# Gate exponentials moved behind the copy of the fourth power, system matrix and attention weights behind the third correction of the inverse

## The reference, cut to what matters

```python
decay = where(tril, exp(g[:, None] - g[None, :]), 0)
M = where(stril, (k_beta @ k.T) * decay, 0)
T = solve_triangular(eye + M, eye, lower=True)
v_c, k_cumdecay = T @ v_beta, T @ (k_beta * exp(g)[:, None])
# over the chunks, one after the other
attn  = (q_i @ k_i.T) * decay_i
v_new = v_i - kcd_i @ state
out_i = (q_i * exp(g_i)[:, None]) @ state + attn @ v_new
state = state * exp(g_last) + (k_i * exp(g_last - g_i)[:, None]).T @ v_new
```

## Time and profile before

| | |
|---|---|
| median of 3 runs | 3789.3 us (3787.47 to 3796.2) |
| profiled execution, its own time | 3785.71 us |
| its span | 3783.8 us |
| busy: PE, DVE, ACT, POOL | 3344.6, 2453.1, 1968.5, 1505.5 us |
| PE weight loads | 2619.3 us |
| granted TensorE clock, mean over the span | 0.982 of full |
| DMA | 261.53 MB, mean 69 GB/s |

### The profile page before, as it was taken

One profiled execution on the slowest core, in us unless ns is written; L12 is line 12 of the kernel. 1 busy time (PEld: TensorE's weight loads), 2 busy tenths in 40 slices (PEclk: granted clock), 3 DMA queues, 4 the chain that ended last, 5 costly groups with the idle time before them and its releaser, 6 DMA issues. The chain is left out here.

```text
span 3783.8 us, 58251 instructions
## 1 busy us (share of the span) xinstructions
PE 3344.6 (88%) x18978; PEld 2619.3 (69%) x18978; DVE 2453.1 (65%) x5143; ACT 1968.5 (52%) x4746; POOL 1505.5 (40%) x2617
## 2 busy tenths in 40 slices
PE   0114999999999999999999999999999999999987
PEld 0113777777777777777777777777777777777763
DVE  6873566666666666666676666666666666666643
ACT  5762555554555555555555555555555555555531
POOL 9963343433433343434344333434333433334310
PEclk9998999999999999999999999999999999999988
DMA  2013222222222222222222222222222122222202
GB/s 95 33 50 135 70 73 73 72 54 71 75 74 64 67 62 76 75 75 69 53 70 77 72 68 72 54 76 76 73 75 70 51 78 70 74 66 66 56 5 100
DMA packets 291213, 261.53 MB, mean 69 GB/s; under 512 B 220992, under 2 KB 249792, under 8 KB 281152
## 3 DMA queue, kind: packets, MB, share of 16 engines
q1 hardware_dynamic: 281696, 123.60, 13.5%
q10 hardware_dynamic: 9216, 134.22, 9.6%
HBM read 228.11 MB, written 29.62 MB: 68 GB/s over the span
## 5 line engine op out<-in xcount | busy, mean ns | idle before, releaser
L638 PE MATMUL x<-xs,w_high 128*128 128x512 f32 x3072 | 1063.4, 427 | 40.0 <-POOL w_low L1229 34.6
L638 PE MATMUL x<-xs,w_low 128*128 128x512 f32 x1536 | 613.6, 399 | 0.0
L873 ACT ACTIVATE uvec<-rb,cpos 128x128 f32<-128x128 f32 x512 | 160.1, 364 | 868.5 <-PE rb L658 868.5
L638 PEld LDWEIGHTS x<-xs,w_high 128*128 128x128 f32 x3072 | 531.3, 193 | 104.5 <-POOL w_low L1229 35.5
L937 ACT ACTIVATE slot<-lane 128x512 fp32r<-128x512 f32 x640 | 350.8, 608 | 402.1 <-PE lane L764 401.7
L1212 POOL TENSOR_TENSOR block_step<-block_in 64x14 f32<-64x14 f32 (+6 forms) x896 | 229.1, 256 | 506.3 <-DMA block_in<-blocks_dram 385.6
L1244 POOL TENSOR_TENSOR rstd<-rarg,powers 128x8 f32<-128x8 f32 x64 | 105.4, 1647 | 625.8 <-DVE rarg L1046 625.8
L638 PEld LDWEIGHTS x<-xs,w_low 128*128 128x128 f32 x1536 | 292.4, 190 | 67.8
L764 PEld LDWEIGHTS lane<-pinv,slot 128*128 128x128 f32 x1536 | 200.2, 192 | 190.2 <-ACT slot L937 98.9
L1009 DVE SCALAR_TENSOR_TENSOR cacc<-x,cwqk,cacc 128x511 f32<-128x511 f32 (+2 forms) x384 | 281.2, 746 | 44.3 <-ACT cacc L860 22.4
L1009 DVE SCALAR_TENSOR_TENSOR cacc<-x,cwv,cacc 128x511 f32<-128x511 f32 (+2 forms) x384 | 281.7, 747 | 37.9 <-ACT cacc L860 4.1
(11 more groups left out here) (203 smaller groups left out, 7737.2 us busy)
## 6 DMA issues: line engine op xcount, KB each, us to landing
xs<-mix_dram ACTq DMA_DIRECT2D x64, 2048.0 KB, 7.7
gb<-cum_dram SPq DMA_DIRECT2D x128, 256.0 KB, 4.4
w_in<-in_w_qkvz SPq DMA_DIRECT2D x48, 512.0 KB, 4.1
w_out<-in_w_out SPq DMA_DIRECT2D x16, 512.0 KB, 4.7
blocks_dram<-bt SPq DMA_DIRECT2D x512, 8.0 KB, 1.5
inverse_dram<-block_out SPq DMA_DIRECT2D x64, 128.0 KB, 2.2
inv<-inverse_dram SPq DMA_DIRECT2D x512, 16.0 KB, 1.8
side_kv<-in_side SPq DMA_DIRECT2D x4, 1024.0 KB, 11.5
```

Of the source, the lines that this page charges most:

```text
L638: ins = mm(PROJ_BANK[kind][i][:, :], w, x, start=(k == 0 and j == 0), stop=(k == KC - 1 and j == 2))
L873: ins = a(uvec[:, h, :], rb[:, sl(h, HD)], ACT.Copy, scale=sm2[p]["cpos"][:, ch, h:h + 1])
```

## The change

ACT: `exp_decay` goes from slot 12 and `exp_small` from slot 13 to slot 14, behind the copy of job 5. DVE: `b_matrix` of both heads goes from slots 13 and 14 to slot 16, behind `finish_product` of job 7 and ahead of that slot's `add_out`; `attention_weights` of head 0 goes from slot 16 to slot 17, beside that of head 1. No instruction is added or taken away.

```diff
@@ -961,9 +961,8 @@
                             silu("qk", l, 1, qkT2[p][:, 0, :])
                         elif k == 9:
                             squares_qk(p)
-                        elif k == 12:
+                        elif k == 14:
                             exp_decay(l)
-                        elif k == 13:
                             exp_small(l, p)
@@ -1163,13 +1162,11 @@
                             conv_tap("qk", l, 1, 3)
                         elif k == 12:
                             small(l, p)
-                        elif k == 13:
+                        elif k == 16:
                             b_matrix(l, 0, p)
-                        elif k == 14:
                             b_matrix(l, 1, p)
-                        elif k == 16:
+                        elif k == 17:
                             attention_weights(l, 0, p)
-                        elif k == 17:
                             attention_weights(l, 1, p)
```

## The result

| | before | after |
|---|---|---|
| median | 3788.61 us (4 runs) | 3955.61 us (3953.68 to 3958.39, 4 runs) |
| ratio, 95% interval | | 1.0437 [1.0419, 1.0455] |
| span of the profiled execution | 3783.8 | 3954.4 |
| mean granted clock of TensorE | 0.982 | 0.946 |

Slower by 167 us, where 46 were forecast (the two profiled executions are 171 us apart). The end of DVE's queue, in the same stretch as the earlier trace rows: corrections of jobs 6 and 7, mask, system matrix, an addition, the attention weights, an addition, job 9.

What follows compares the result with a forecast made beforehand. PE's queue was taken to set the time of some 62 equal passes. DVE's queue cost 43 us and the blocks' inversion 3, sum 46: 3789.3 + 46 = 3835 us, slower by 1.2%; 8-in-10 range 3806 to 3872.

Steps and rivals of the forecast that it cites:

- The move on ACT: Exponentials behind ACT's copy of job 5 let job 6 start earlier in each pass: a gain of 1.35 us.
- The queue on DVE: DVE's work from job 7's pair to job 9's, 7.57 us, makes job 10 late; a pass loses 0.7 us.
- the 60 to 110: Sign to look for: PE's waits for DVE ahead of job 10, 60 to 110 us in all.
- The stall on `lower`: POOL's `lower` slows the system matrix's second four tiles on DVE; the 3.21 us for eight tiles was kept.
- The inversion of the blocks: Chain from head 1's `b_ready` to next pass's job 0 loses 4.55 us of slack; ten passes stall, 3 us.
- The rival's reason: Rival (chance 0.13), inversion chain becomes the bound, 3863 us; against it, a gather not beside `xs`'s load may be quicker.
- The clock: Rival (chance 0.05): PE's new wait ahead of job 10 brings more drops to the lower clock, 30 us, 3865 us.
- the 43 of the queue: Main term: 0.7 us lost per pass to DVE's queue ahead of job 9, over 62 passes.
- the eleven falls: Eleven passes of about 53.0 us with TensorE's clock at 1.2 GHz for a while, costing 1.5 us each.
- the rival: The clock rival (chance 0.05): every third pass falls once more, 20 x 1.5 = 30 us on top, 3865 us.

Runs made afterwards that it cites:

- e2: Only DVE's half of the change (system matrix behind job 7), ACT's order as in the kernel before: 3962.08 us, ratio 1.0472.
- e5: Changed kernel with head 0's decays, mask and four matrix tiles back at their old places, head 1's left moved: 3743.96 us, ratio 0.9882.
- e3: Changed kernel plus eight unused 128x512 products in PE's wait ahead of job 10: 3853.81 us, ratio 1.0177.
- e11: Changed kernel plus four unused 128x512 products in PE's wait ahead of job 10: 3854.77 us, ratio 1.0175.
- e4: Kernel before plus three unused 128x512 products between the last output product and job 10: 3845.24 us, ratio 1.0162.
- e10: Kernel before plus eight unused 128x512 products between the last output product and job 10: 3970.81 us, ratio 1.0481.
- e6: Changed kernel with a quarter of z's projection moved between the key sums and the heads' transposes: 3890.85 us, ratio 1.0265.
- e8: Kernel before with a quarter of z's projection moved between the key sums and the heads' transposes: 3791.96 us, ratio 1.0009.
- e1: Only ACT's half of the change (exponentials behind the copy of job 5), DVE's order as in the kernel before: 4175.44 us, ratio 1.1031.

## Why the prediction was wrong, point by point

- *The move on ACT*: right. Job 6 follows 1.75 us behind job 5, a gain of 1.29 (1.35 forecast), and PE's waits for ACT's copy are gone.
- *The queue on DVE*: right. 7.48 us against 7.57; job 10 is 0.73 late against 0.82; PE's waits for L1107 add up to 105.2 us, inside the 60 to 110. A clean pass is 0.6 to 0.7 us longer, as forecast. e2's clean 53.2 and e5's clean 50.0 came from the same working.
- *The stall on `lower`*: right, it came along (3.21 us for eight tiles), and e5 shows what it costs: 0.9.
- *The inversion of the blocks*: it was no loss to speak of. Job 0 comes late in four passes, by 0.1 to 0.3 us, where ten by 0.1 to 0.7 were forecast: under 1 us in all instead of 3. The falls behind job 10 don't hide more, since e3, which has none, shows three late passes, by 0.2 to 0.5 us. The way from the matrix's end to POOL's first step, 8.3 us in the one pass of the earlier trace rows, got quicker: over all 64 its median is 7.11 us before and 6.90 after, its mean 7.38 and 6.96, and 14 passes took over 7.8 us before and one after. The rival's reason, that the gather no longer runs beside the load of `xs`, fits this, but no run tests it.
- *The clock*: here it failed. The work came out as summed, some 40 us for the 43 of the queue. The prediction took the eleven falls as a constant, and sized the rival as "if every third pass fell once more, 20 x 1.5 = 30 us", with 0.05. It was 89 falls more, 132 us. Two things were wrong in that step. The wait ahead of job 10 was set beside the 0.72 us ahead of job 6, which made no fall; at 1.68 us it is followed by one in 39 of 61 passes (e3 and e11 take them away). And the larger part, 50 more falls behind the key sums, was not thought of at all: the eleven came in the trace at distances of five to seven passes, and the change altered the length of the pass. e4 and e10 show that the length alone moves their number, and the even distances of the falls in e2 fit two rhythms that shift against each other. Of where the second comes from no run says anything.

What stays open: how the 61 falls behind the key sums divide. With the wait filled and the same clean length there are 32 and 30 (e3, e11); the other 30 or so come along with the falls behind job 10, which lengthen the pass further, but no run changes the one and holds the other. What in the products ahead of a fall makes it is open too; e6 and e8 only show that one dense quarter between key sums and transposes is not enough.

## What to carry to other kernels

A correction moved ahead in one engine's queue pays only as far as what was moved behind it still fits before the next deadline: add up the queue between the two deadlines, and use the hole that the move opens. When the profile shows the granted clock falling in some iterations of a loop and not in others, don't take their number as fixed: any edit that changes the length of the loop, a gain too, can change it several times over, and the price of one fall (1.5 us here) times all iterations belongs in the range. To know what is work and what is clock, compare iterations without a fall.

## What the runs showed of the hardware

- Extra work made a kernel faster: 504 products of 128x512 in an idle stretch of PE took 102 us off (3955.61 to 3853.81).
- The same loop without a single new wait had 11, 30 or 55 falls of the clock in 61 passes when its clean length was 51.5, 52.1 or 53.3 us. At 50.0 us there were 45. There is no direction in it: shorter was worse than 51.5 as well.
- A wait of PE of 1.7 us was followed by a fall in 39 of 61 passes in one kernel and in 2 in another (e2); a wait of 0.7 to 0.8 us in none. In a wait of 4.6 us the clock fell while PE was still empty, in all 61 (e1).
- Falls in a row came at an even 54.61 us, though the passes between them were 54.7 to 54.8 us long (e2).
